# Layer 0's last results mixed into the rows beside the end of attention, seven of eight additions on POOL, and an unread Gelu behind each pair of roots

## The chip, the cores and the metric

The kernel runs on one core of a Trainium2 chip. The core has five engines, each with its own instruction queue: PE (TensorE, matrix products, with PEld for its weight loads), DVE (VectorE, elementwise and reductions), ACT (ScalarE, functions from tables and copies), POOL (GpSimd, elementwise work in SBUF and indirect DMAs), and SP (SyncE, which here only issues DMAs). An engine runs its queue in order; engines wait for each other on semaphores. The metric is the device time of one execution in microseconds (us), lower is better.

## What is computed

Two layers on 4 x 1024 rows of 256 numbers (4096 tokens), all in f32. In the reference, cut to what matters:

```
xn = layernorm(x)
s  = window attention(xn)             # 16 heads, windows of 64, relative bias, projection
g  = silu(xn + top-1 of 32 experts(xn))   # capacity 160 rows each
x  = x + s * g
xn = layernorm(x)
s  = unbind(cumsum(bind(keys, values)), query)  # unit spectra of xn Wk, xn Wv, xn Wq by FFT
g  = silu(top-2 of 8 experts(xn))     # hidden 1024, Gelu
x  = x + s * g
```

`x = x + s * g` of layer 0 and the layer norm behind it are the place of one part of the change. The other part lies where layer 1's experts (Gelu) run beside the magnitudes of the spectra (square roots).

## The kernel before

The rows lie in SBUF as 32 tiles of 128 tokens x 256, and the work between the layers goes by **quarters** of 4 tiles: there are `QUARTERS` = 8 of them, so a quarter is four tiles and not a fourth of the rows. `X` holds the rows, `XN` the normalized rows (its memory is lent to the experts' rows and down weights meanwhile), `S` the attention's output.

**The order.** `schedule0` writes one list, `plan0`, of named pieces for layer 0 and the passage to layer 1, and every engine's function walks the same list and issues its own share of each piece. What follows a product (`pt_out`, `even`, `odd`, `share`) is entered with a lag counted in PE columns (`later`), and `need` puts it in ahead of who reads it. The main loop runs over 64 window steps `s` (`STEPS`; 128 query rows each, all heads): scores for two steps at a time, `pturn(s)` (PE turns the probabilities), `pv(t)` for two steps, `proj(t)`. `side` deals the pieces of the 32 experts in between: rows turned, `gu` (gate and up products), `down`, and a `tail` for the last 32 rows of each of four experts. Their pace is set by `FIRST_EXPERT_STEP` = 9 and `LAST_EXPERT_STEP` = 62. Softmax of one step is shared out: DVE adds the bias and takes the maximum (L1509, L1513), POOL subtracts it (L2336), ACT takes Exp (L2152), DVE sums (L1523), POOL divides (L2343).

**The passage.** Each expert's result is scattered by POOL to `mixed_dram` (L2354). When all 40 scatters have landed, SP loads the mixed rows back by quarters (`mix_load`, L2531), ACT takes Silu in place (`mix_silu`, L2205), DVE multiplies by S (`mix_mul`, L1585) and adds to X (`mix_sum`, L1590). `stats` (L1349, L1351, L1354 on DVE, then a root on ACT, L2070) and `norm` (L1359, L1361, and one tile in four L1365 on DVE, three on ACT, L2215) follow. `combination` sets their order: quarter q's turn is statistics of q + 1, product and sum of q + 2, norm of q; then PE turns the quarter and starts layer 1's spectra. All of it stands behind the end of attention. Behind the last quarter comes the routing of layer 1, a chain of small operations, most of them on DVE, each waiting for the one before.

**Layer 1.** `schedule1` writes `plan1`: 39 slots of expert work (`w1`, L1308, with Gelu by chunk on ACT, L2284; `w2`, L1318), one or two tiles of 128 rows each; the slots of one tile stand among the first. Beside them go the 16 chunks of the spectra: `magnitudes` takes the root of two chunks at a time (L2258), `squares` squares the next chunk (L2251). Roots and Gelus are in different function tables, and the build puts an ACT_TABLE_LOAD ahead of the first operation that needs another table. Three PSUM banks take W1's chunks: the product of chunk c + 3 waits for the Gelu of chunk c. `gelu_table` is an unread Gelu of one column, already used once, ahead of the first slot.

Of the kernel before, what the change touches and what calls it, by code (L numbers as in the profile page):

```python
# [6 lines left out]
ALU = mybir.AluOpType  # L7
# [6 lines left out]
NT = T // P  # L14
# [116 lines left out]
UNITS, UW, UT, SR, PR0, STEPS = NT // 2, 4, 2 * P, 2, 4, 2 * NT  # L131
QUADS, RR = PAIRS // 2, 4
QUARTERS = NT // 4
EARLY_STEPS, FIRST_EXPERT_STEP, LAST_EXPERT_STEP = 8, 9, 62
NB, ROW, TOKEN, GATE = D + 1, D + 2, D, D + 1
TAIL, TAILS_AT, DOWNS, YS = CAP - P, GROUP, 6, 4
EXPERT_PIECES = GT + 2 * E0
# [71 lines left out]
def schedule0(banks):  # L209

    order = Order(banks)
# [173 lines left out]
    def spectrum(ch, n, lag):  # L385
        order.product("spectrum", ch, n, bank=spectrum_bank(ch, n), columns=0, then=[("spectrum_out", lag)])

    def combination():
        add("load_wf")
        for q in range(QUARTERS):  # L390
            add("mix_load", q)
            add("mix_silu", q)
        for q in range(2):
            add("mix_mul", q)
            add("mix_sum", q)
            if q == 0:
                add("stats", 1, 0)
        for q in range(QUARTERS):
            g = 4 * q
            if q and q % 2 == 0:  # L400
                need(("route1_turn_out", g - 8))
            if q + 1 < QUARTERS:
                add("stats", 1, g + 4)
            if q + 2 < QUARTERS:
                add("mix_mul", q + 2)
                add("mix_sum", q + 2)
            add("norm", 1, g)
            if q:
                need(("spectrum_out", *SPECTRA_AHEAD[q - 1]))
            turn(1, g, 4)  # L410
            if q % 2 == 0 and q:
                route1_turn(g - 8)
            spectrum(*SPECTRA_AHEAD[q], LATER)
            if q % 2:
                route1(g - 4)
        need(("spectrum_out", *SPECTRA_AHEAD[QUARTERS - 1]))
        route1_turn(4 * QUARTERS - 8)
        need(("route1_turn_out", 4 * QUARTERS - 8))
# [11 lines left out]
                pieces[0] += 1  # L430

    start()
    for s in range(STEPS + 4):
        u, g = divmod(s, UW)
        if s + 2 < STEPS:
            if s % 2 == 0:
                scores(s // 2 + 1)
            scored(s + 2)
        if u + 1 < UNITS and g < 3:
            (q, k, v)[g](u + 1)  # L440
        side(2 * s)
        if s % 2 == 0 and 0 <= s - 2 < STEPS:
            pv((s - 2) // 2)
        if s % 2 and 0 <= s - 3 < STEPS:
            proj((s - 3) // 2)
        side(2 * s + 1)
        if s < STEPS:
            pturn(s)
    assert next(ffn, None) is None and next(route, None) is None
    order.settle(order.clock + STEPS * UT)  # L450
    combination()
    order.settle(order.clock + STEPS * UT)
    return order.plan
# [21 lines left out]
def schedule1(banks):  # L475
# [77 lines left out]
    for n in range(NSLOT):  # L553
# [10 lines left out]
                    add("magnitudes", later)  # L564
        if ch + 2 < CHUNKS:
            spectra(ch + 2)
        for due in weights_due:
            add("load_weights", due)
        weights_due = []
# [60 lines left out]
def build(nc, a, out):  # L630
# [701 lines left out]
    def vector(e):  # L1332
        w = Waits(e)
# [68 lines left out]
        for what, *at in plan0:  # L1402
# [163 lines left out]
            elif what == "row_tokens":  # L1566
                grp, = at
                wait_rows0(w, grp)
                e.tensor_copy(row_token0[:, grp, :], rows0[:, row_slot(grp, 0):row_slot(grp, 0) + GT, TOKEN]).then_inc(
                    row_tokens_ready, 1)  # L1570
            elif what in ("y_out", "tail_out"):
                n, = at
                grp, t = divmod(n, GROUP) if what == "y_out" else (n, TAILS_AT)
                u = use["down", n] if what == "y_out" else use["tail", n]
                i = y_turn(grp, t) % YS
                rows = rows0[:, row_slot(grp, t), :]
                filled_by(u)
                w.wait_ge(y_out[i], 16 * (y_turn(grp, t) // YS))
                e.scalar_tensor_tensor(out=y0[:, i, :], in0=PS[:, u.bank, 0:D], scalar=rows[:, GATE:GATE + 1],  # L1579
                                       in1=rows[:, 0:D], op0=ALU.mult, op1=ALU.add).then_inc(free[u.bank], 1)  # L1580
            elif what == "mix_mul":
                q, = at
                four = slice(4 * q, 4 * q + 4)
                w.wait_ge(gated0, q + 1)
                e.tensor_tensor(S[:, four, :], XN[:, four, 0:D], S[:, four, :], ALU.mult).then_inc(scaled0, 1)  # L1585
            elif what == "mix_sum":
                q, = at
                four = slice(4 * q, 4 * q + 4)
                w.wait_ge(scaled0, q + 1)
                e.tensor_tensor(X[:, four, :], X[:, four, :], S[:, four, :], ALU.add).then_inc(x1_ready, 1)  # L1590
# [715 lines left out]
    def gpsimd(e):  # L2306
# [11 lines left out]
        for what, *at in plan0:  # L2318
# [27 lines left out]
            elif what in ("y_out", "tail_out"):  # L2346
# [8 lines left out]
                    out=mixed_dram, out_offset=bass.IndirectOffsetOnAxis(ap=row_token0[:, grp, t:t + 1], axis=0),  # L2355
                    in_=y0[:, i, :], in_offset=None, bounds_check=T - 1, oob_is_err=False).then_inc(y_out[i], 16)

        def late_put(n, j):
            tile = 2 * (n - EARLY) + j
            w.wait_ge(late_ready, tile + 1 if n == LAST else tile - j + 2)  # L2360
            wait_stored(w, QUARTERS)
            w.wait_ge(selected, 2)
            e.indirect_dma_start(
                out=out, out_offset=bass.IndirectOffsetOnAxis(ap=put_of[:, tile:tile + 1], axis=0), in_=fin[:, tile, 0:D],
                in_offset=None, bounds_check=T - 1, oob_is_err=False).then_inc(late_stored, 16)
# [294 lines left out]
```

## Time and profile before

| | us |
|---|---|
| median of 3 timed runs | 1129.23 (1128.43 to 1129.9) |
| the profiled execution, its own time | 1124.32 |
| its span in the trace | 1122.5 |

| engine | busy us | share of the span |
|---|---|---|
| PE | 1027.6 | 92% |
| PEld | 883.9 | 79% |
| DVE | 692.4 | 62% |
| ACT | 531.8 | 47% |
| POOL | 404.1 | 36% |

The mean granted clock of PE is 0.968 of full speed. Times within the trace count from the span's start. Attention of layer 0 with its experts ends at about 418 us, the passage to layer 1 at about 475, routing at about 545; the rest is layer 1's experts and spectra. A row of a timeline gives start, duration, engine, line, operation, what it writes and reads, how many instructions were merged, and in brackets the idle time before it with what ended it. Durations overlap a little, since an engine takes up an instruction before the one ahead has quite ended.

### The profile page before, as it was taken

The numbers are of one execution on the slowest core, as the hardware profiler recorded it, in microseconds if no ns is written. First come the engines' busy times: TensorE is split into PE (matmuls) and PEld (weight loads), VectorE is DVE, ScalarE is ACT, GpSimd is POOL, SyncE is SP. The second block draws the span as 40 slices with busy tenths as digits, with TensorE's granted clock in tenths as the row PEclk, the third lists the DMA queues.
The fourth block names the chain that finished last, engine by engine and source line by source line (L and its number), as shares of the span: only waits on it lengthen the run. The fifth ranks groups of instructions, "written<-read, shape, count | busy, mean of one in ns | idle before, by whom it ended". The sixth has DMA issues, their size and how long they took to land.

```text
span 1122.5 us, 16791 instructions
## 1 busy us (share of the span) xinstructions
PE 1027.6 (92%) x6152; PEld 883.9 (79%) x6152; DVE 692.4 (62%) x1488; ACT 531.8 (47%) x1101; POOL 404.1 (36%) x385
## 2 busy tenths in 40 slices
PE   3876999999999984789999999999999999999995
PEld 2665788888888863578888898988888888888884
DVE  7777876777777759588845644474765200058853
ACT  4624655555555536743444545455453223356531
POOL 1056545454555440000243322332231245522364
PEclk9969999999999996987999999999999999999998
DMA  9932345546565338426496855544234579989971
GB/s 307 287 136 81 94 134 164 171 133 190 179 210 174 103 109 264 157 93 254 98 350 241 290 188 187 185 171 188 108 130 191 213 269 340 338 294 389 390 285 63
DMA packets 120401, 228.65 MB, mean 204 GB/s; under 512 B 14938, under 2 KB 103914, under 8 KB 115328
## 3 DMA queue, kind: packets, MB, share of 16 engines
q1 hardware_dynamic: 106448, 189.31, 48.7%
q0 software_dynamic: 13872, 38.27, 10.3%
q8 instruction: 49, 0.80, 0.3%
q14 instruction: 32, 0.26, 0.1%
HBM read 166.98 MB, written 62.79 MB: 205 GB/s over the span
## 4 chain that ended last, share of the span: by engine, by line
PE 72%; DVE 14%; ACT 5%; issue 3%; POOL 2%; DMA 2%; SPq 0%; POOLq 0%; DVEq 0%; ACTq 0%
PE PS L1318 20%; PE PS L1308 20%; PE PS L1207 6%; PE PS L1092 4%; PE PS L1042 4%; PE PS L1146 3%; PE PS L1217 2%; PE PS L1173 2%; PE PS L1101 2%; PE PS L1159 2%; PE PS L1184 2%; POOL table L2327 2%; DVE stats L1349 2%; PE PS L1294 1%; DVE hot_tile L1831 1%
## 5 line engine op out<-in xcount | busy, mean ns | idle before, releaser
L1308 PE MATMUL PS<-xgT,WE 128*128 128x256 f32 (+1 forms) x1248 | 254.7, 361 | 5.0 <-ACT hT L2284 4.3
L2284 ACT ACTIVATE hT<-PS,WE 128x256 f32<-128x256 f32 (+1 forms) x312 | 140.2, 455 | 227.0 <-PE PS L1308 224.1
L1308 PEld LDWEIGHTS PS<-xgT,WE 128*128 128x128 f32 x1248 | 219.3, 190 | 33.3 <-ACT hT L2284 6.6
L1318 PE MATMUL PS<-WE,hT 128*128 128x256 f32 x1104 | 244.6, 379 | 0.0
L1318 PEld LDWEIGHTS PS<-WE,hT 128*128 128x128 f32 x1104 | 207.4, 190 | 27.0
L1943 DVE TENSOR_TENSOR y<-PS,WE 128x512 f32<-128x512 f32 (+1 forms) x38 | 24.3, 640 | 211.1 <-PE PS L1318 211.1
L2384 POOL DMA_INDIRECT xg<-xn_dram,token_of x71 | 74.2, 1045 | 136.9 <-DVE result_of L1859 115.1
L2396 POOL DMA_INDIRECT result<-y,result_of x53 | 53.7, 1013 | 175.7 <-DVE y L1943 168.5
L1042 PE MATMUL PS<-XT,Wf 128*128 128x256 f32 x384 | 91.6, 393 | 3.3 <-ACT Z L2061 3.3
L1042 PEld LDWEIGHTS PS<-XT,Wf 128*128 128x128 f32 x384 | 73.7, 197 | 14.6 <-ACT Z L2061 4.9
L2343 POOL TENSOR_TENSOR prob<-prob,row_sum 128x512 f32<-128x512 f32 x56 | 58.6, 1046 | 59.5 <-DVE row_sum L1525 59.2
L1207 PE MATMUL PS<-rowsT,wgu 128*128 128x160 f32 x512 | 75.6, 301 | 0.0
L2336 POOL TENSOR_TENSOR sc<-sc,sc_max 128x512 f32<-128x512 f32 x56 | 58.5, 1046 | 42.5 <-DVE sc_max L1513 42.1
L1207 PEld LDWEIGHTS PS<-rowsT,wgu 128*128 128x128 f32 x512 | 71.9, 190 | 2.3 <-issue 1.4
L1092 PE MATMUL PS<-XT,qkv_w 128*128 128x256 f32 x256 | 65.6, 402 | 0.0
L1031 PE MATMUL PS<-const,XN 128*128 128x128 f32 x128 | 27.0, 347 | 40.2 <-DVE XN L1365 38.1
L2372 POOL TENSOR_TENSOR MAG<-SQ 128x768 f32<-128x768 f32 x13 | 25.3, 1945 | 99.0 <-ACT SQ L2251 99.0
L1523 DVE TENSOR_REDUCE row_sum<-prob 128x8 f32<-128x512 f32 x64 | 43.5, 680 | 28.0 <-ACT prob L2152 27.3
L1031 PEld LDWEIGHTS PS<-const,XN 128*128 128x128 f32 x128 | 18.0, 171 | 50.1 <-issue 21.7
L2354 POOL DMA_INDIRECT mixed_dram<-y,row_token x40 | 39.7, 993 | 47.4 <-DVE y L1579 42.9
L1092 PEld LDWEIGHTS PS<-XT,qkv_w 128*128 128x128 f32 x256 | 48.6, 200 | 8.1 <-issue 0.6
L2162 ACT ACTIVATE PT<-PS 128x512 f32<-128x512 f32 x64 | 38.4, 600 | 32.2 <-PE PS L1159 31.1
(280 smaller groups left out, 1714.4 us busy)
## 6 DMA issues: line engine op xcount, KB each, us to landing
WE<-in_experts SPq DMA_DIRECT2D x39, 2180.0 KB, 9.7
wgu<-in_w_gate SPq DMA_DIRECT2D x32, 256.0 KB, 2.9
wgu<-in_w_up SPq DMA_DIRECT2D x32, 256.0 KB, 3.2
wdn<-in_w_down SPq DMA_DIRECT2D x32, 256.0 KB, 3.9
result<-zeros SPq DMA_DIRECT2D x16, 512.0 KB, 5.0
xs<-late_dram SPq DMA_DIRECT2D x16, 512.0 KB, 13.5
both<-result SPq DMA_DIRECT2D x16, 512.0 KB, 8.3
table<-zeros POOLq DMA_DIRECT2D x1, 5160.0 KB, 31.1
```

The costliest lines, as they stand in the source:

```text
L1031: m = e.transpose(out_v[:, k, j * P:(j + 1) * P], XN[:, 2 * pair + j, k * P:(k + 1) * P], ident)
L1042: m = e.matmul(PS[:, u.bank, part * CH:(part + 1) * CH], Wf[:, n, k, part * P:(part + 1) * P], XT1[:, ch, k, :], start=k == 0, stop=k == K ...
L1092: m = e.matmul(PS[:, u.bank, c * UT:(c + 1) * UT], qkv_w[:, k, col:col + P], XT0[:, unit, k, :], start=k == 0, stop=k == KD - 1)
L1207: m = e.matmul(PS[:, u.bank + f, n * CAP:(n + 1) * CAP], wgu0[:, ex % 2, n, k, f * P:(f + 1) * P], rowsT[:, grp % 2, k, j * CAP:(j + 1) * ...
L1308: m = e.matmul(PS[:, FIRST_H_BANK + nth % HR, 0:rows], W1[n % WR][:, k, c * P:(c + 1) * P], xgT[:, n % 2, k, 0:rows], start=k == 0, stop=k ...
L1318: m = e.matmul(PS[:, u.bank, j * D:(j + 1) * D], hT[:, n % 2, c, j * P:(j + 1) * P], W2[n % WR][:, c, :], start=c == 0, stop=c == KF - 1)
L1523: e.tensor_reduce(row_sum[:, s % RR, :], prob[:, s % PR0, :, :], AX.X, ALU.add).then_inc(row_sum_done, 1)
L2284: e.activation(hT[:, n % 2, c, 0:rows], PS[:, FIRST_H_BANK + (KF * n + c) % HR, 0:rows], ACT.Gelu_apprx_tanh, bias=b1[n % WR][:, c:c + 1], ...
L2336: e.tensor_tensor(by_head, by_head, sc_max[:, s % SR, :].unsqueeze(2).to_broadcast([P, PAIRS, WIN]), ALU.subtract).then_inc(sc_sub_done, 1)
L2343: e.tensor_tensor(prob[:, s % PR0, :, :], prob[:, s % PR0, :, :], row_sum[:, s % RR, :].unsqueeze(2).to_broadcast([P, PAIRS, WIN]), ALU.mu ...
L2384: e.indirect_dma_start(out=xg[:, n % XR, j, :], out_offset=None, in_=xn_dram, in_offset=bass.IndirectOffsetOnAxis(ap=token_of[:, tile:tile ...
L2396: e.indirect_dma_start(out=result1, out_offset=bass.IndirectOffsetOnAxis(ap=result_of[:, tile:tile + 1], axis=0), in_=y1[:, n % YR, j, :], ...
```

## The change

The pace of the experts ends at step 60 in place of 62. The loads of the mixed rows, their Silus, the first quarter's product, sum and statistics, and the second quarter's product move into a new function, `attention_end`, which lies around the last `proj`, `pv` and `proj`. DVE adds quarter 0 alone; POOL adds quarters 1 to 7, behind its last work of layer 0. `gelu_table` is put behind the squares of each odd `ch` from 3 to 15, seven times.

```
-EARLY_STEPS, FIRST_EXPERT_STEP, LAST_EXPERT_STEP = 8, 9, 62
+EARLY_STEPS, FIRST_EXPERT_STEP, LAST_EXPERT_STEP = 8, 9, 60
...
-    def combination():
+    def attention_end():
         add("load_wf")
         for q in range(QUARTERS):
             add("mix_load", q)
+        proj(NT - 2)
+        need(("pt_out", STEPS - 1))
+        add("mix_silu", 0)
+        pv(NT - 1)
+        need(("even", NT - 1))
+        for q in range(1, QUARTERS):
             add("mix_silu", q)
-        for q in range(2):
-            add("mix_mul", q)
-            add("mix_sum", q)
-            if q == 0:
-                add("stats", 1, 0)
+        need(("odd", NT - 1))
+        add("mix_mul", 0)
+        add("mix_sum", 0)
+        add("stats", 1, 0)
+        proj(NT - 1)
+        need(("s_out", NT - 1))
+        add("mix_mul", 1)
+        add("mix_sum", 1)
+
+    def combination():
...
+        if ch % 2 and 1 < ch < CHUNKS:
+            add("gelu_table")
...
             elif what == "mix_sum":
                 q, = at
+                if q:
+                    continue
...
+        for q in range(1, QUARTERS):
+            four = slice(4 * q, 4 * q + 4)
+            w.wait_ge(scaled0, q + 1)
+            w.wait_ge(x1_ready, q)
+            e.tensor_tensor(X[:, four, :], X[:, four, :], S[:, four, :], ALU.add).then_inc(x1_ready, 1)
```

The main loop now ends at step 63 and not four steps later, and nothing is settled between it and `attention_end`. Line numbers of the changed kernel are 12 to 20 higher than before in the engines' functions.

**PE at the end of attention.** 1217 or 1229 is the down product, 1227 or 1239 the tail, 1159 or 1171 a `pturn`, 1173 or 1185 a `pv`, 1184 or 1196 a `proj`. Before, from the last `pturn` ahead of the tail on:

```order
L1159 MATMUL PS<-const,prob 128x128 x4
L1173 MATMUL PS<-PT,VB 64x2x64 x8
L1217 MATMUL PS<-wdn_111,hT_109 128x256 x2
L1227 MATMUL PS<-wdn_111,hT_109 32x256 x8
L1159 MATMUL PS<-const,prob 128x128 x4
L1184 MATMUL PS<-proj_w,OT 128x256 x2
L1159 MATMUL PS<-const,prob 128x128 x4
L1173 MATMUL PS<-PT,VB 64x2x64 x8
L1184 MATMUL PS<-proj_w,OT 128x256 x2
```

And now:

```order
L1229 MATMUL PS<-wdn_111,hT_109 128x256 x2
L1239 MATMUL PS<-wdn_111,hT_109 32x256 x8
L1171 MATMUL PS<-const,prob 128x128 x4
L1196 MATMUL PS<-proj_w,OT 128x256 x2
L1171 MATMUL PS<-const,prob 128x128 x4
L1185 MATMUL PS<-PT,VB 64x2x64 x8
L1171 MATMUL PS<-const,prob 128x128 x8
L1196 MATMUL PS<-proj_w,OT 128x256 x2
L1185 MATMUL PS<-PT,VB 64x2x64 x8
L1196 MATMUL PS<-proj_w,OT 128x256 x2
```

Two `pturn`s, a `proj` and a `pv` that stood ahead of the last down product now stand behind the tail.

**POOL at the same place.** Before, its last work of layer 0 was:

```order
L2354 DMA mixed_dram<-y_102,row_token_52 4096x256
L2336 TENSOR_TENSOR sc<-sc,sc_max 128x512
L2343 TENSOR_TENSOR prob<-prob,row_sum 128x512 x2
L2354 DMA mixed_dram<-y_102,row_token_52 4096x256 x3
L2384 DMA xg<-xn_dram,token_of 128x256 x7
```

And now:

```order
L2350 TENSOR_TENSOR sc<-sc,sc_max 128x512
L2368 DMA mixed_dram<-y_102,row_token_52 4096x256 x2
L2350 TENSOR_TENSOR sc<-sc,sc_max 128x512
L2357 TENSOR_TENSOR prob<-prob,row_sum 128x512 x2
L2376 TENSOR_TENSOR X<-X,S 128x1024 x7
L2404 DMA xg<-xn_dram,token_of 128x256 x7
```

The last two scatters stand ahead of the last subtraction and the last two divisions, and the seven sums follow these.

**DVE in one turn of the loop over quarters** (the product of one quarter up to the statistics of the same). Before:

```order
L1585 TENSOR_TENSOR S<-XN,S 128x1024
L1590 TENSOR_TENSOR X<-X,S 128x1024
L1359 RECIPROCAL rstd<-rstd 128x4
L1361 SCALAR_TENSOR_TENSOR shift<-mean_var,rstd 128x4
L1365 TENSOR_SCALAR XN<-X,mean_var,rstd 128x256
L1349 BN_STATS stats<-X 128x6
```

And now:

```order
L1597 TENSOR_TENSOR S<-XN,S 128x1024
L1371 RECIPROCAL rstd<-rstd 128x4
L1373 SCALAR_TENSOR_TENSOR shift<-mean_var,rstd 128x4
L1377 TENSOR_SCALAR XN<-X,mean_var,rstd 128x256
L1361 BN_STATS stats<-X 128x6
```

The sum is gone from DVE, and the statistics behind the norm now read what POOL has added.

## Rows read from the trace of the kernel before

**Rows 1.** Stages: from:to, length, busy us of each engine (instructions), granted clock, DMA share, GB/s
```profile
445.00:455.00 10.00, 7.99 (x50) 5.26 (x50) 9.56 (x27) 6.53 (x16) 0.00 (x0) 1.00 0.62 211
...
570.00:850.00 280.00, 273.31 (x1430) 242.09 (x1429) 157.98 (x295) 134.03 (x273) 88.11 (x76) 1.00 0.55 201
```

**Rows 2.** Timeline of PE, end of attention: start, duration, line, operation, count, idle time before
```profile
409.02 1.10 PE L1173 MATMUL PS<-PT,VB 128*64 128x128 f32 x16 [0.69 <-ACT PT L2162]
...
412.11 0.66 PE L1159 MATMUL PS<-const,prob 128*128 128x128 f32 x4
412.60 1.03 PE L1184 MATMUL PS<-proj_w,OT 128*128 128x256 f32 x4
413.47 0.60 PE L1159 MATMUL PS<-const,prob 128*128 128x128 f32 x4
```

**Rows 3.** Timeline of POOL: the last steps' softmax, and the last scatter
```profile
405.72 1.05 POOL L2336 TENSOR_TENSOR sc<-sc,sc_max 128x512 f32<-128x512 f32 x1
...
408.93 1.04 POOL L2343 TENSOR_TENSOR prob<-prob,row_sum 128x512 f32<-128x512 f32 x1 [1.16 <-DVE row_sum L1525]
...
413.74 0.97 POOL L2354 DMA_INDIRECT mixed_dram<-y,row_token  x1 [0.30 <-issue]
```

**Rows 4.** Timeline of ACT: end of attention, first Silu, root of the last quarter
```profile
412.80 0.60 ACT L2162 ACTIVATE PT<-PS 128x512 f32<-128x512 f32 x1 [2.16 <-PE PS L1159]
...
415.90 0.48 ACT L2172 ACTIVATE OT<-PS,const 128x256 f32<-128x256 f32 x1 [1.19 <-PE PS L1173]
416.39 1.28 ACT L2205 ACT_TABLE_LOAD   x1
420.48 1.06 ACT L2205 ACTIVATE XN<-XN 128x1024 f32<-128x1024 f32 x1 [2.80 <-DMA XN<-mixed_dram]
...
465.99 0.20 ACT L2070 ACTIVATE rstd<-rstd 128x4 f32<-128x4 f32 x1
```

**Rows 5.** Timeline of DVE, the loop over quarters: quarters 0, 1 and 7
```profile
421.56 1.22 DVE L1585 TENSOR_TENSOR S<-XN,S 128x1024 f32<-128x1024 f32 x1 [3.03 <-ACT XN L2205]
...
424.08 0.43 DVE L1349 BATCH_NORM_STATS2 stats<-X 128x6 f32<-128x256 f32 x1
...
426.42 1.22 DVE L1585 TENSOR_TENSOR S<-XN,S 128x1024 f32<-128x1024 f32 x1
...
457.93 1.22 DVE L1585 TENSOR_TENSOR S<-XN,S 128x1024 f32<-128x1024 f32 x1
...
460.32 0.17 DVE L1359 RECIPROCAL rstd<-rstd 128x4 f32<-128x4 f32 x1
```

**Rows 6.** Two-input operations on POOL: the page's costliest groups, then line 2372 (min/median/max)
```profile
L2336 POOL TENSOR_TENSOR sc<-sc,sc_max 128x512 f32<-128x512 f32 x56 | 58.5, 1046 | 42.5 <-DVE sc_max L1513 42.1
...
L2372 POOL TENSOR_TENSOR MAG<-SQ x13: 1793/1803/2340, 551.9 to 830.7; 128x768 f32<-128x768 f32 x13
```

**Rows 7.** Timeline of PE, W1 of two one-tile slots: with a table load, without one
```profile
590.34 1.50 PE L1308 MATMUL PS<-xgT,WE 128*128 128x128 f32 x12
592.77 2.50 PE L1308 MATMUL PS<-xgT,WE 128*128 128x128 f32 x20 [0.92 <-ACT hT L2284]
...
613.92 3.74 PE L1308 MATMUL PS<-xgT,WE 128*128 128x128 f32 x32
```

**Rows 8.** Timeline of PE, W1 of two two-tile slots: with a table load, without one
```profile
751.36 2.76 PE L1308 MATMUL PS<-xgT,WE 128*128 128x256 f32 x12
754.31 4.58 PE L1308 MATMUL PS<-xgT,WE 128*128 128x256 f32 x20 [0.20 <-ACT hT L2284]
...
772.15 7.07 PE L1308 MATMUL PS<-xgT,WE 128*128 128x256 f32 x32
```

**Rows 9.** Timeline of ACT around the Gelu table load of one slot
```profile
586.07 1.65 ACT L2251 ACTIVATE SQ<-Z 128x512 f32<-128x512 f32 x3
591.06 1.28 ACT L2284 ACT_TABLE_LOAD   x1 [3.34 <-PE PS L1308]
592.35 0.88 ACT L2284 ACTIVATE hT<-PS,WE 128x128 f32<-128x128 f32 x3
```

## What I expected, before the changed kernel ran

> **What bounds the kernel now.** I read the table of stages first, then each engine's timeline at the three places that the edit touches. In layer 1's part PE is busy 273.3 of 280 us, so there whatever makes PE wait counts in full [rows 1]. In the passage between the layers DVE is busy 9.56 of 10 us and PE, ACT and POOL are not: POOL does nothing at all there [rows 1]. DVE starts a quarter's product at 421.56, the next at 426.42 and the product of quarter 7 at 457.93, which is 5.25 us a quarter over the last six [rows 5]. Before the passage the path is a string of single events: the last scatter is issued at 413.74, the first quarter has landed and its Silu starts at 420.48 (6.74 later), and DVE's product starts 1.08 after that [rows 3, 4, 5]. Behind the passage comes the routing of layer 1, small operations that wait for each other, so a shift of the passage's end goes through to the end of the kernel.
>
> **The change, part 1: the start of the passage.** What PE does is the same, in another order. Behind the tail now also stand two `pturn`s, a `proj` and a `pv`: 2 x 0.49 (412.11 to 412.60), 0.87 (412.60 to 413.47), 1.10 and the 0.69 that this `pv` waits for ACT's copy, in all 3.64 us [rows 2]. A `pturn`'s successor starts at 412.11 right behind the tail, so the tail ends at about 412.1 - 3.6 = 408.5. The last scatter came 1.63 after the tail (412.11 to 413.74) [rows 2, 3] and so is now issued at about 410.1; the first quarter could be there at 410.1 + 6.74 = 416.8.
>
> It can't be used then. On POOL the last subtraction and the last two divisions are queued behind the two scatters. The scatter ends at about 411.1 (0.97). From the start of a subtraction to the end of the same step's division it is 405.72 to 409.97, 4.25 us [rows 3], so the last division ends at about 411.2 + 4.25 = 415.5. Then come `pturn` (PE to the start of ACT's copy: 412.11 to 412.80, 0.69) and the copy, 0.60, which end at 416.8 [rows 2, 4]. The first Silu is behind this copy on ACT and needs a table load of 1.28 [rows 4], so it starts at about 418.1, with the data long there. Behind it, and not ahead, stands `even` of the last tile, and the product on DVE is behind `odd`: 1.08 + 0.48 + 0.48 (`odd` taken at `even`'s length) [rows 4]. Product 0 starts at about 420.2, 1.4 earlier than before. Product 1 now also has the last `s_out` ahead of it, at most another 0.48: it starts at 426.42 - 1.4 + 0.5 = 425.5, 0.9 earlier. The two steps of head start shrink to that.
>
> **Part 2: a turn of the loop.** DVE gives up a sum. From the start of a product to the first statistics it was 2.52 for product and sum, so 1.26 each; the statistics up to the next product take 2.34 (424.08 to 426.42) [rows 5]. But the order on DVE is: product of q + 2, norm of q, statistics of q + 2. The statistics read the sum, which POOL can only begin when the product is done, and DVE has only the norm to do meanwhile. So a turn becomes 1.26 + P + 2.34 + about 0.1 for two hand-overs (my estimate, an idle time of some hundredths at each) = 3.70 + P, with P the time of one sum of 1024 numbers a partition on POOL. The trace has no such operation. The nearest rows: 512 numbers, one operand broadcast, 1.046 us, twice that is 2.09; and 768 numbers with two full operands, median 1.803, times 4/3 is 2.40 [rows 6]. I take the middle, 2.25. As the upper end, the slowest of the thirteen, 2.340 for 768, gives 3.12 [rows 6]. The turn is then 5.95 us in place of 5.25. The wait that replaces the sum costs more than the sum.
>
> What is queued behind that wait: all of DVE, and through it ACT's three tiles of each norm and PE's turns and spectra. One thing comes earlier: the norm of a quarter no longer has the sum ahead of it, so it stands at 2.39 - 1.26 = 1.13 behind the product (before: 457.93 to 460.32) [rows 5]. Product 7 starts at 425.5 + 6 x 5.95 = 461.2 and the norm behind it at 462.3, against 460.32: **+2.0 us**. In general the shift is 6P - 11.5: +1.0 at 2.09, +2.9 at 2.40, +7.2 at 3.12. From there on ACT and PE carry the chain, up to the root of the last quarter at 465.99 [rows 4]; its statistics are ready at 425.5 + 7 x (3.70 + P) = 467.2, still ahead of that root (465.99 + 2.0 = 468.0). Only from P = 3.1 on do they come last, and the shift is then 7P - 14.6.
>
> The Trainium skill, "GPSIMD Engine Reference", section "Elementwise — side-by-side cycle accounting", gives 4497 ns for an f32 add of 2048 numbers on POOL; half of it, an estimate, is 2.25, which is what the rows above bracket, and by the page the sum comes out as here.
>
> **Part 3: the unread Gelus.** In a slot that follows roots, the load of the Gelu table stands ahead of the first Gelu and behind its wait for PE: ACT has been idle for 3.34 us, then loads from 591.06 to 592.35 [rows 9]. PE's product of chunk 4 waits for that Gelu. In one-tile slots W1 takes 590.34 to 595.27, 4.93 us, against 3.74 without a load: 1.19 [rows 7]. In two-tile slots 751.36 to 758.89, 7.53, against 7.07: 0.46 [rows 8]. By the slots' order the seven places fall on three one-tile and four two-tile slots: 3 x 1.19 + 4 x 0.46 = **5.4 us**. The load moves behind the squares, which end at 587.7 here; load and unread Gelu (1.28 and about 0.2, by the root of four columns, 0.20) end by 589.3, ahead of the first chunk at 591.06 [rows 4, 9]. What hides it is PE's W2 ahead of the slot. If that cover were gone, each would cost what it costs now, so this part has no loss in it. PE waits for nothing else at these seven places.
>
> The Trainium skill, "ScalarE: Activation LUTs", section "What ACT_TABLE_LOAD costs", counts 1283 ns for the load and 1380 more for a drain. The row shows the Gelu start 1.29 us after the load began [rows 9], so the trace agrees with the first number and shows nothing of the second.
>
> **Part 4: the pace of the experts.** The pieces stand closer by 51/53 and PE does the same work at the same total. I put it at nothing, and keep 1 us on either side for where a `pturn` may meet a later softmax.
>
> **Sum.** +2.0 - 5.4 = -3.4 us, the span 1119.1 in place of 1122.5, the profiled execution 1120.9 in place of 1124.32. That execution was 4.9 us below the median of the timed runs; I take the difference off the median: 1129.23 - 3.4 = **1125.8**. A measurement of this kernel can tell about 0.2% (2.3 us) from no change.
>
> **Rivals.**
> *POOL's sum is quick enough to count as small.* At P = 2.09 the shift is +1.0 and the total -4.4: 1124.8. It is the lower side of the forecast, with 1 us of part 4 beyond it: 1123.8.
> *The gain of the Gelus is eaten.* If P lies between 2.44 and 3.18 (6P - 16.9 above -2.3, 7P - 20.0 below +2.3), or part 4 costs its 1 us at P = 2.3, the kernel is within 0.2%. For it: full operands cost 2.35 ns a number against 2.04 [rows 6]. At 3.12: +7.2 - 5.4 = +1.8, 1131.0.
> *The unread Gelus do nothing*, because PE's gain comes back as a wait on the spectra's chain on DVE. Then +2.0 stays: 1131.2, still within 0.2%. Against it: PE has no wait on DVE in these slots, and DVE is busy 158 of 280 us [rows 1].
> *Slower: POOL and DVE take turns at SBUF.* DVE's norm and ACT's normalization run beside POOL's sum, which has two operands from SBUF. If a sum takes twice the broadcast row's time per number, P = 4.18, the shift is 7 x 4.18 - 14.6 = +14.7 and the total +9.3: 1138.5. It decides from P = 3.18 on. Against it: the sums of squares run in slots where DVE works too, and half of the thirteen lie between 1.793 and 1.803 [rows 6]. The Trainium skill, "GPSIMD Engine Reference", section "Key points", says that POOL's SBUF interfaces are shared with DVE and contended when DVE reads two SBUF operands; the loop has such an operation on DVE only while POOL has no sum, so by that rule the sums would be little disturbed.
>
> **How the numbers follow.** The forecast (P up to 2.44, Gelus pay) 0.56. Within 0.2%: P up to 3.18 or part 4 against me 0.20, Gelus that do nothing 0.12. Slower 0.12. So faster 0.56, same 0.32, slower 0.12. The range goes from 1123.8 less a little, 1123.6, to the case of the idle Gelus, 1131.2; the slow case is left out, with a few hundredths below.
>
> **What would show it.** In the new profile: POOL's seven sums and their mean (2.25 by me, and which P decides); DVE's products 5.95 us apart with an idle time of 1.5 to 1.7 in each turn that ends with POOL; first product at 420.2 and not 418; the first Silu behind a table load at 416.8; the norm behind product 7 at 462.3. In layer 1 no table load at the Gelus' line, and W1 at 3.74 and 7.07 in all slots. I am wrong if the turn stays below 5.3 us, if the last divisions on POOL don't hold back the Silu, or if PE shows a new wait in the slots.

## The result, and the profile after

The changed kernel is slower: a median of 1136.82 us (7 runs, 1132.95 to 1139.95) against 1128.71 for the kernel before, taken beside it (7 runs), a ratio of 1.0076 with a 95% interval of [1.006, 1.0092]. I had forecast 1125.8 and a range of 1123.6 to 1131.2. Its profiled execution took 1135.17 us, with a span of 1133.4 in place of 1122.5, so the two traces differ by 10.9 us.

The table says where, worked out from starts and ends in the two traces. "Expert" is PE's first product of layer 0's experts (L1207, after L1219), "tail" the end of the last tail (L1227, after L1239), "product" DVE's S<-XN,S of a quarter, "routing" the first operation of layer 1's routing.

| stretch, us | before | after | difference | forecast |
|---|---|---|---|---|
| start to first expert | 134.13 | 133.97 | -0.2 | 0 |
| first expert to tail | 278.05 | 279.80 | +1.75 | -3.6 |
| tail to product 0 | 9.38 | 14.38 | +5.0 | +2.3 |
| product 0 to product 1 | 4.86 | 5.18 | +0.3 | +0.4 |
| product 1 to product 7 | 31.51 | 37.16 | +5.65 | +4.2 |
| product 7 to routing | 17.66 | 19.63 | +2.0 | -1.25 |
| routing to the end | 646.91 | 643.28 | -3.6 | -5.4 |

The table of stages, from:to, length, busy us of PE, PEld, DVE, ACT and POOL (instructions), granted clock, DMA share, GB/s, to be held against [rows 1]:

```profile
445.00:455.00 10.00, 7.71 (x43) 5.07 (x41) 9.69 (x19) 4.65 (x12) 4.26 (x2) 0.88 0.50 173
570.00:850.00 280.00, 276.32 (x1461) 246.32 (x1460) 158.25 (x299) 139.25 (x287) 89.05 (x77) 1.00 0.55 202
```

DVE gave up a sum in each turn and is as busy as before, 9.69 of 10 us; its instructions in the window fall from 27 to 19. A busy engine that issues fewer instructions spends longer in some of them. In layer 1's part PE goes from 273.31 to 276.32 busy: there the unread Gelus did what was said of them.

**The end of the attention**, first PE, then POOL, then ACT, in the changed kernel (start, duration, engine, line, operation, count, idle time before and what ended it), to be held against [rows 2 to 4]:

```profile
412.70 1.07 PE L1239 MATMUL PS<-wdn,hT 128*32 128x256 f32 x16
413.71 0.66 PE L1171 MATMUL PS<-const,prob 128*128 128x128 f32 x4
...
416.35 1.09 PE L1185 MATMUL PS<-PT,VB 128*64 128x128 f32 x16 [0.69 <-ACT PT L2176]
418.73 0.66 PE L1171 MATMUL PS<-const,prob 128*128 128x128 f32 x4 [1.28 <-POOL prob L2357]
422.67 1.11 PE L1171 MATMUL PS<-const,prob 128*128 128x128 f32 x4 [3.28 <-POOL prob L2357]
423.57 1.91 PE L1196 MATMUL PS<-proj_w,OT 128*128 128x256 f32 x4
```

```profile
415.63 0.97 POOL L2368 DMA_INDIRECT mixed_dram<-y,row_token  x1 [0.30 <-issue]
416.62 1.06 POOL L2350 TENSOR_TENSOR sc<-sc,sc_max 128x512 f32<-128x512 f32 x1
417.62 1.05 POOL L2357 TENSOR_TENSOR prob<-prob,row_sum 128x512 f32<-128x512 f32 x1
421.57 1.04 POOL L2357 TENSOR_TENSOR prob<-prob,row_sum 128x512 f32<-128x512 f32 x1 [2.90 <-DVE row_sum L1537]
```

```profile
419.42 0.60 ACT L2176 ACTIVATE PT<-PS 128x512 f32<-128x512 f32 x1 [1.46 <-PE PS L1171]
419.92 0.62 ACT L2166 ACTIVATE prob<-sc 128x512 f32<-128x512 f32 x1
423.82 0.60 ACT L2176 ACTIVATE PT<-PS 128x512 f32<-128x512 f32 x1 [3.28 <-PE PS L1171]
424.43 1.28 ACT L2219 ACT_TABLE_LOAD   x1
425.73 1.06 ACT L2219 ACTIVATE XN<-XN 128x1024 f32<-128x1024 f32 x1
```

POOL's subtraction for the last step waits behind two scatters, as I had worked out. What I had not seen is on ACT: the Exp that follows it (419.92) is ready at 417.7 and stands behind the copy of the step before (419.42), which waits for a `pturn`, which waits for the division of that step. From the start of a subtraction to the end of its step's division it took 4.25 us [rows 3] and takes 5.99 here (416.62 to 422.61). PE has nothing else left, idles for 1.28 and 3.28 us, and then works slower: a `pturn` of four goes from 0.66 to 1.11, a `proj` from 1.03 to 1.91. The granted clock was 0.70 from 418 to 423 us and 0.62 from 423 to 428, between its two levels, full speed at 2.4 GHz and half of it at 1.2.

**A turn of the loop.** DVE from one product to the next, and POOL's sum beside it, to be held against [rows 5]:

```profile
439.33 1.22 DVE L1597 TENSOR_TENSOR S<-XN,S 128x1024 f32<-128x1024 f32 x1
440.47 0.17 DVE L1371 RECIPROCAL rstd<-rstd 128x4 f32<-128x4 f32 x1
440.67 2.32 DVE L1373 SCALAR_TENSOR_TENSOR shift<-mean_var,rstd 128x4 f32<-128x4 f32 x1
442.91 0.40 DVE L1377 TENSOR_SCALAR XN<-X,mean_var,rstd 128x256 f32<-128x256 f32 x1
443.23 0.41 DVE L1361 BATCH_NORM_STATS2 stats<-X 128x6 f32<-128x256 f32 x1
...
445.55 1.22 DVE L1597 TENSOR_TENSOR S<-XN,S 128x1024 f32<-128x1024 f32 x1
```

```profile
440.63 2.34 POOL L2376 TENSOR_TENSOR X<-X,S 128x1024 f32<-128x1024 f32 x1 [3.67 <-DVE S L1597]
```

The product is followed by an operation on four numbers a partition that takes 2.32 us; the sum on POOL starts 0.04 before it and ends at 442.97, with it (442.99). The turn is 6.22 us. The seven sums take 2.337 to 2.354 us. The norm, held back with the shift, still stands ahead of the statistics when the sum has ended (442.97), so these start 0.26 us behind it, at 443.23. POOL's own line says that DVE waited for it once, for 2.5 us; in the other six turns the wait is inside the four-column operation, where a table of waits doesn't show it.

**The unread Gelus.** ACT around one of the seven in the changed kernel, and PE's W1 of the two slots behind it, to be held against [rows 7 to 9]:

```profile
602.15 1.65 ACT L2265 ACTIVATE SQ<-Z 128x512 f32<-128x512 f32 x3
603.82 1.28 ACT L2268 ACT_TABLE_LOAD   x1
605.12 0.20 ACT L2268 ACTIVATE shift<-shift 128x1 f32<-128x1 f32 x1
607.16 1.18 ACT L2298 ACTIVATE hT<-PS,WE 128x128 f32<-128x128 f32 x3 [1.84 <-PE PS L1320]
```

```profile
606.43 3.74 PE L1320 MATMUL PS<-xgT,WE 128*128 128x128 f32 x32
...
613.89 7.07 PE L1320 MATMUL PS<-xgT,WE 128*128 128x256 f32 x32
```

Load and unread Gelu are over 1.1 us before W1 begins, and W1 runs through in 3.74 and 7.07 us.

### The profile page after: what moved, and what is told of

The parts are those of the page before. It is cut to its first block, busy times and chain, and to the rows that moved or that the text cites. A ratio compares the mean times of both kernels' runs of the same rounds, so it can differ in the third digit from the quotient of the medians.

```text
span 1133.4 us, 16797 instructions
## 1 busy us (share of the span) xinstructions
PE 1030.8 (91%) x6152; PEld 886.7 (78%) x6152; DVE 697.5 (62%) x1481; ACT 534.5 (47%) x1108; POOL 419.8 (37%) x392
## 4 chain that ended last, share of the span: by engine, by line
PE 70%; DVE 15%; ACT 4%; issue 4%; POOL 4%; DMA 2%; SPq 1%; POOLq 0%; DVEq 0%; ACTq 0%
PE PS L1320 20%; PE PS L1330 20%; PE PS L1219 5%; PE PS L1054 4%; PE PS L1104 3%; PE PS L1158 2%; POOL table L2341 2%; PE PS L1113 2%; PE PS L1229 2%; PE PS L1185 2%; PE PS L1196 2%; PE PS L1171 2%; DVE stats L1361 1%; DVE shift L1373 1%; PE PS L1306 1%
## 5 line engine op out<-in xcount | busy, mean ns | idle before, releaser
L1054 PE MATMUL PS<-XT,Wf 128*128 128x256 f32 x384 | 94.5, 402 | 3.3 <-ACT Z L2075 3.3
L1219 PE MATMUL PS<-rowsT,wgu 128*128 128x160 f32 x512 | 75.6, 301 | 0.0
L1219 PEld LDWEIGHTS PS<-rowsT,wgu 128*128 128x128 f32 x512 | 72.0, 190 | 2.4 <-issue 1.4
```

What stands on the lines that cost most here:

```text
L1054: m = e.matmul(PS[:, u.bank, part * CH:(part + 1) * CH], Wf[:, n, k, part * P:(part + 1) * P], XT1[:, ch, k, :], start=k == 0, stop=k == K ...
L1219: m = e.matmul(PS[:, u.bank + f, n * CAP:(n + 1) * CAP], wgu0[:, ex % 2, n, k, f * P:(f + 1) * P], rowsT[:, grp % 2, k, j * CAP:(j + 1) * ...
```

## The experiments

Three questions: which part costs what; what holds DVE beside POOL's sums; and whether POOL's help can pay in another order. The measure in the traces is the **passage**, from the tail's end to the first routing operation: 63.41 us before, 76.35 after. It does not contain the start of the program, which varies: the first expert product stands between 134 and 144 us in the traces, so spans and times contain a difference that none of the edits made.

### The Gelus alone, the pace alone, POOL's sums alone

```
# gelu_only: the kernel before, and
+        if ch % 2 and 1 < ch < CHUNKS:
+            add("gelu_table")
# pace_only: the kernel before, and
-EARLY_STEPS, FIRST_EXPERT_STEP, LAST_EXPERT_STEP = 8, 9, 62
+EARLY_STEPS, FIRST_EXPERT_STEP, LAST_EXPERT_STEP = 8, 9, 60
# pool_only: the kernel before, "if q: continue" in DVE's mix_sum, and the loop of seven sums on POOL
```

> The kernel before with the seven unread Gelus alone. Theory: they pay in full also here, 5.4 us (3 x 1.19 + 4 x 0.46) less than before, with W1 at 3.74 us in one-tile slots and 7.07 in two-tile slots, and no table load at the Gelus' line. Rival: the gain seen behind the changed passage is owed to another state of the spectra there, and alone they give back 1 us or nothing.

> The kernel before with the experts' pace at step 60 alone; the passage stays behind all of attention. Theory: the denser pieces make PE wait in mid-attention (rows not yet landed, OT, keys), about 3 to 5 us more idle time between 95 us and the tail than before, and because attention also ends on softmax steps without experts' work to lie beside, the passage starts 3 to 6 us later. Rival: the pace costs nothing, the last scatter goes out 3 us earlier than before, and all that was lost at the end of attention comes from the new order of Silu and attention.

> The kernel before with the sums of quarters 1 to 7 on POOL alone. Theory: products of the loop stand 6.23 us apart in place of 5.25, as in the changed kernel, product 7 comes 5.9 later, and with the later norm behind it the passage ends 7 to 8 us later; the DVE operation that makes the shift takes 2.3 us in each turn, as long as the sum beside it. Rival: the loop's price hangs on the early start (DMAs of the mixed rows still landing), and here it is under 3 us.

| against 1127.83 before | median us | ratio, 95% | passage | routing to the end |
|---|---|---|---|---|
| Gelus | 1123.04 | 0.9966 [0.9952, 0.998] | 63.80 | 641.97 |
| pace | 1134.35 | 1.0058 [1.0042, 1.0075] | 69.85 | 648.62 |
| POOL's sums | 1138.85 | 1.0101 [1.0078, 1.0124] | 71.20 | 648.72 |

In microseconds, by the ratio and its interval: the Gelus give 3.8 [2.3, 5.4] (4.8 in the medians); the pace, which I had put at nothing, costs 6.5 [4.7, 8.5] by itself; POOL's sums cost 11.4 [8.8, 14] (11.0 in the medians). Of these 11.4 the passage shows 7.8 (71.20 - 63.41); the rest I can't place in one trace. With POOL's sums alone the same operation on four columns takes as long as in the changed kernel:

```profile
439.28 2.31 DVE L1361 SCALAR_TENSOR_TENSOR shift<-mean_var,rstd 128x4 f32<-128x4 f32 x1
```

For the pace, the waits of PE between 134 and 414 us (what, line, waited for; us in total, times, longest), in the kernel before and then with the pace alone:

```profile
PE PS L1173 <- ACT PT L2162: 0.7, 1, 0.7
PE PS L1184 <- DVE OT L1536: 0.2, 1, 0.2
PE PS L1146 <- DVE KB L1485: 0.2, 1, 0.2
```

```profile
PE PS L1184 <- DVE OT L1536: 2.0, 2, 1.3
PE PS L1192 <- DMA rows<-table: 1.9, 2, 1.4
PE PS L1146 <- DVE KB L1485: 0.4, 1, 0.4
PE PS L1184 <- DVE KB L1485: 0.3, 1, 0.3
PE PS L1092 <- ACT Q L2093: 0.2, 1, 0.2
```

From the first expert on they grow from 1.1 to 4.6 us (the last row of the second view lies ahead of it). Closer pieces ask for a gathered tile (rows<-table), for a `proj`'s input and for keys before these are there, at six places of the attention. The other part is at the end: with the tail two `pturn`s, a `proj` and a `pv` further ahead, tail to product is 15.81 us, where 9.38 and the 3.64 us of moved work would be 13.0. The changed kernel, with its own order at the end, waits for the same four things in the attention (2.0, 1.9, 0.4 and 0.4). The share of the gathered tiles is not in every execution: `after_dve` below has the same pace and none of it, and its way from the first expert to the tail is 277.58 us.

### The new end alone, and the changed kernel with the old pace

```
# end_only: attention_end and the loop to STEPS as in the changed kernel; no Gelus, sums on DVE, and
# pace_back: the changed kernel, and
-EARLY_STEPS, FIRST_EXPERT_STEP, LAST_EXPERT_STEP = 8, 9, 60
+EARLY_STEPS, FIRST_EXPERT_STEP, LAST_EXPERT_STEP = 8, 9, 62
```

> The kernel before with the loads, Silus and first products placed around the last steps of attention, the pace left at 62, all sums on DVE, no unread Gelus. Theory: with the old pace the last scatters are no earlier than before, so the start of the first product moves by at most 1 us either way, and the kernel is within 1.5 us of before. Rival: placing Silu ahead of the last attention output costs 3 us or more by itself, because the last head outputs wait behind it on ACT.

> The changed kernel with the pace put back to step 62, all else kept. Theory: the pace costs twice, by PE's waits between the first expert and the tail (4.7 us in place of 1.2) and by the two scatters that stand ahead of the last subtraction on POOL; put back, the first product comes 10.4 us behind the tail in place of 14.4 and the tail 1.3 earlier, so the kernel is 5 to 6 us faster than the changed one. Rival: the long way from the tail to the first product is owed to the Silu placed between attention's last steps, then it stays at 13 or more.

The new end alone: 1130.88 us, 1.0019 [1.0, 1.0039], passage 64.72. The changed kernel with the old pace: 1132.17 against 1128.31, 1.0029 [1.0009, 1.0049], passage 72.64 in place of 76.35. So the new end by itself costs 1.3 us in the trace (tail to product 0 10.36, product 0 to 1 5.18, since the second product now has the last `s_out` ahead of it), and by the ratio 2.1 [0, 4.4], where 1.5 at most was expected. Put back, the pace returns some 5.3 us, give or take 3 (1.0076 to 1.0029), of the 8.6 that the changed kernel lost: a large part of the loss was in the part that I gave two sentences. The prices of the four single edits don't add up to the whole: 6.5 + 11.4 + 2.1 - 3.8 = 16.2 us against 8.6. One overlap is seen in the traces: pace alone and end alone lengthen tail to product 0 by 6.4 and 1.0 us, and both together, in the changed kernel, by 5.0.

### What holds DVE: another shift, and a sum with one operand

`shift_apart` is the changed kernel with the four-column operation cut into four of one column, each with one tensor from SBUF and one number a partition. `pool_one` is the kernel before with, in place of the seven sums, a product of X with 1 on POOL; it leaves out the addition of S to quarters 1 to 7.

```
# shift_apart
-            e.scalar_tensor_tensor(out=shift[:, g:g + n], in0=mean_var[:, g:g + n, 0], scalar=-1.0, in1=rstd[:, g:g + n],
-                                   op0=ALU.mult, op1=ALU.mult).then_inc(ln_shift, 1)
+            for t in range(g, g + n):
+                m = e.tensor_scalar(shift[:, t:t + 1], mean_var[:, t, 0:1], rstd[:, t:t + 1], -1.0, ALU.mult, ALU.mult)
+            m.then_inc(ln_shift, 1)
# pool_one, against pool_only
-            e.tensor_tensor(X[:, four, :], X[:, four, :], S[:, four, :], ALU.add).then_inc(x1_ready, 1)
+            e.tensor_scalar(X[:, four, :], X[:, four, :], 1.0, None, ALU.mult).then_inc(x1_ready, 1)
```

> The changed kernel with the norm's shift made by four DVE operations that read one column each as a scalar (one SBUF operand) in place of one operation with two operands from SBUF. Theory: a DVE operation with two SBUF operands cannot start while POOL's two-operand sum runs; without it the norm ends 2 us earlier, products stand 6.0 us apart in place of 6.2 and the passage ends 3 us earlier. Rival: whatever DVE does first beside a POOL sum takes 2.3 us, or the operation waits for something else; then the first of the four takes 2.3 us and nothing moves.

> The kernel before, with POOL's seven sums replaced by a multiplication of X by 1 in place (one operand from SBUF, same size); the addition of S to quarters 1 to 7 is left out. My theory: DVE is held by POOL's two operands from SBUF. With one operand DVE's 4-column shift operation, which took 2.31 us beside a sum, takes 0.16 to 0.3, and the norm is not held; the loop's turn is 3.70 us plus the time of this POOL operation plus about 0.15. Rival: any POOL operation of that size holds DVE: then the shift operation again lasts until POOL's operation ends. Second rival: the shift operation waits for something else in the new order (a root, a semaphore): then it is 2 us again too, whatever POOL does.

DVE and POOL in the kernel with the shift apart (1136.38 us, 1.0066 [1.0046, 1.0086]):

```profile
447.77 0.58 DVE L1374 TENSOR_SCALAR shift<-mean_var,rstd 128x1 f32<-128x1 f32 x4
448.27 1.96 DVE L1378 TENSOR_SCALAR XN<-X,mean_var,rstd 128x256 f32<-128x256 f32 x1
```

```profile
447.73 2.34 POOL L2377 TENSOR_TENSOR X<-X,S 128x1024 f32<-128x1024 f32 x1 [3.67 <-DVE S L1598]
```

The shift is free of the sum (0.58 for four), and now the next operation is held, the one of 256 columns, 1.96 us where it takes 0.40 alone, though it reads one tensor of that width and two numbers a partition. So two tensors are not the only form that is held, which neither expectation had. The shift being ready sets ACT's three tiles free, and product 7 to routing is back at 17.68; the turn only falls to 6.03, since the statistics read the sum anyway. In the trace the passage gains 2.7 us (73.63); in time the two kernels can't be told apart.

And the one with a single operand on POOL, DVE first:

```profile
444.32 1.01 DVE L1361 SCALAR_TENSOR_TENSOR shift<-mean_var,rstd 128x4 f32<-128x4 f32 x1
445.26 0.40 DVE L1365 TENSOR_SCALAR XN<-X,mean_var,rstd 128x256 f32<-128x256 f32 x1
```

```profile
444.29 2.77 POOL L2364 TENSOR_SCALAR X<-X 128x1024 f32<-128x1024 f32 x1 [3.67 <-DVE S L1585]
```

Neither expectation holds as written. The operation is held for 0.85 us and let go 1.7 us before POOL has ended, and the norm behind it takes its usual 0.40 with POOL still at work. So the hold depends on what POOL does, and it is no semaphore and no root; but one operand on POOL also holds DVE for a while. Why just so long stays open, and so does whether the number of operands decides or the kind of operation, since the run changed both. The turn, 3.70 us plus POOL's time, comes out here: 3.70 + 2.77 = 6.47, measured 6.45 (38.67 / 6). Beside the sums it is 6.19 and not 6.04: there the held norm delays the statistics. In time this kernel is 1148.46 against 1137.14, 1.009 [1.006, 1.012]; its rows are other ones behind the passage, so only the loop is read from it.

### The changed kernel with its sums back on DVE

```
# after_dve: the changed kernel without "if q: continue" and without the seven sums on POOL
```

> The changed kernel with all sums on DVE again (pace 60, the new end of attention and the seven Gelus stay). My theory: the turn of the loop goes back from 6.19 to 5.25 us and the norm behind product 7 is not held, so 5.65 + 2.0 = 7.6 us come back: about 1129.2 against the 1136.8 of the changed kernel, within 0.2% of the kernel before; what stays is the pace and the new end (+6.5) against the Gelus (-5). Rival: the longer turn comes from the later start of the passage or from the order around it, not from POOL: then the product 0 to product 7 stretch stays at 42 us and the time above 1134.

1136.59 us against 1137.14, 0.9996 [0.9977, 1.0015] (`after_dve`, `pool_one` and `ahead_dve_gelu` ran on another chip, where the kernel before takes 1137.14 us, so only their ratios are compared). The changed kernel stands at 1.0076, so in it POOL's sums cost about 0.8%, 9 us, give or take 3. The turn is 5.25 us again and product 7 to routing 17.67, which gives back the 7.6 expected. The passage is 69.43 in place of 76.35, 6.9 us less, since tail to product 0 is 0.7 longer in this trace. What stays against the kernel before is the pace and the end, +6.0 in the passage; in time the Gelus about pay for it.

### The loop in another order, with POOL's sums and without

The turn is long because the statistics of a quarter stand right behind its sum. Here a quarter's product is issued three quarters ahead and its statistics one turn later, so that POOL adds while DVE does another quarter's statistics. Start, pace and end of attention are those of the kernel before, and the Gelus are in.

```
-        for q in range(2):
+        for q in range(3):
             add("mix_mul", q)
             add("mix_sum", q)
-            if q == 0:
-                add("stats", 1, 0)
+            if q:
+                add("stats", 1, 4 * q - 4)
...
-            if q + 1 < QUARTERS:
-                add("stats", 1, g + 4)
-            if q + 2 < QUARTERS:
-                add("mix_mul", q + 2)
-                add("mix_sum", q + 2)
             add("norm", 1, g)
+            if q + 3 < QUARTERS:
+                add("mix_mul", q + 3)
+                add("mix_sum", q + 3)
...
             spectrum(*SPECTRA_AHEAD[q], LATER)
+            if q + 2 < QUARTERS:
+                add("stats", 1, g + 8)
```

`ahead_gelu` has the sums on POOL, `ahead_gelu_shift` also the shift apart, `ahead_dve_gelu` has all sums on DVE.

> The kernel before with the unread Gelus and POOL's sums, but the loop reordered: norm of q, product of q + 3, statistics of q + 2, so that a sum lies beside statistics of another quarter. Theory: statistics have one SBUF operand and are not held by POOL's sum, and no one waits for the sum; a turn takes 1.2 + 0.6 + 2.3 = 4.1 to 4.4 us in place of 5.25, the passage ends about 5 us earlier than before, and with the Gelus the kernel is 9 to 11 us faster than before. Rival: statistics stretch beside the sum as the shift does, a turn stays above 5.2 us and only the Gelus' 5.4 us are left.

> As the reordered kernel with the unread Gelus, and the shift from four operations with one SBUF operand each. Theory: the sum ends about when the statistics do, so there is little left to free; within 1 us of the other. Rival: sums still overlap the next norm by 0.5 us or more a turn, then this one is 2 to 4 us faster.

> The reordered loop (product two quarters further ahead, statistics a quarter behind the sum) with all sums on DVE, and the seven Gelus. My theory: DVE is the bound of the loop, so without POOL's help the turn stays at about 5.25 us whatever the order, products 1 to 7 take 31.5 us and the time is that of the Gelus alone, 1122 to 1124: the gain of 4.3 us of the reordered loop with POOL's sums comes from the sums that DVE doesn't do. Rival: the order alone does it (statistics further from the norm, ACT and PE less late): then turns near 4.7 us or a time of 1119 to 1120.

| | median us | before | ratio, 95% | product 1 to 7 | passage |
|---|---|---|---|---|---|
| sums on POOL | 1118.76 | 1128.31 | 0.9923 [0.9908, 0.9938] | 26.94 | 58.97 |
| and shift apart | 1121.40 | 1128.31 | 0.9943 [0.993, 0.9957] | 29.01 | 59.67 |
| sums on DVE | 1130.77 | 1137.14 | 0.9936 [0.9912, 0.996] | 31.50 | 63.25 |

One turn of the first, DVE and POOL:

```profile
440.98 0.16 DVE L1363 SCALAR_TENSOR_TENSOR shift<-mean_var,rstd 128x4 f32<-128x4 f32 x1
441.06 0.41 DVE L1367 TENSOR_SCALAR XN<-X,mean_var,rstd 128x256 f32<-128x256 f32 x1
441.38 1.22 DVE L1587 TENSOR_TENSOR S<-XN,S 128x1024 f32<-128x1024 f32 x1
442.52 0.42 DVE L1351 BATCH_NORM_STATS2 stats<-X 128x6 f32<-128x256 f32 x1
...
445.19 0.16 DVE L1363 SCALAR_TENSOR_TENSOR shift<-mean_var,rstd 128x4 f32<-128x4 f32 x1
...
445.59 1.22 DVE L1587 TENSOR_TENSOR S<-XN,S 128x1024 f32<-128x1024 f32 x1
```

```profile
442.68 2.37 POOL L2366 TENSOR_TENSOR X<-X,S 128x1024 f32<-128x1024 f32 x1 [1.84 <-DVE S L1587]
```

This turn is 4.21 us (4.49 on average, since the second of the six is 6.57). The statistics run beside the sum at their usual 0.4 us, and the shift falls behind its end, at 0.16. There the shift apart has nothing to free and only adds: four operations take 0.58 us where one takes 0.16, the turn is 4.62, and products 1 to 7 take 2.1 us longer, where I had expected the two kernels within 1 us. With the sums on POOL and the shift whole this is the version that beats both kernels: 9.6 us below the kernel before, and by the intervals better than the Gelus alone (0.9952 to 0.998). The expected 9 to 11 us came, with 4.4 of passage. In the traces the order alone brings 0.5 us of passage (63.80 to 63.25) and POOL's sums in it another 4.3 (58.97). The times don't show that split: the intervals with and without POOL overlap, and the two ran on different chips.

## Why the prediction was wrong

**Where PE, DVE and POOL stand** (what bounds the kernel now): right. DVE bounds the passage, and its shift goes through to the end.

**Part 1, the start of the passage: wrong by 8.1 us**, from the first expert to product 0: 279.80 + 14.38 = 294.18, where I had 420.2 - 134.13 = 286.07. I named the queue on POOL rightly: last scatter 1.86 us behind the tail (1.63 said), the divisions held back, the Silu behind the last copy and a table load. Three terms were missing or too small. From the first expert the tail comes 5.4 us later than I said: 3.5 are PE's new waits, which belong to part 4, 0.9 is a `proj` that stood ahead of the first expert and now stands behind it, and 1.0 I can't place. The step of 4.25 from subtraction to division was read from a place where ACT was free; here the Exp was queued behind a copy that waited for PE: +1.75. And I priced PE's last pieces at full clock: from the end of the division to product 0 it is 5.54 us (422.61 to 428.15) in place of 4.7, because the copy starts 1.15 behind its `pturn` and not 0.69, and `even` waits 0.46 for the slower `pv`. The chain of one step must be read with what stands ahead of each of its links on its own engine.

**Part 2, the loop.** The turn, 3.70 + P with P = 2.25, came out as 6.19 with P = 2.34: nearly right in form (3.70 + 2.34 is 6.04, the held norm makes the rest), and 1.5 us too small over six turns, within the bounds I had. The term that failed is the one behind it: "the norm of a quarter no longer has the sum ahead of it, so it stands at 1.13 behind the product". It stands 3.58 behind (439.33 to 442.91), because DVE's shift is held for as long as POOL adds. That turned a gain of 1.25 us into a loss of 2.0. This was to be read before the run: in the trace of the kernel before, DVE and then POOL at two places of layer 1 where both read two tensors from SBUF:

```profile
551.83 0.42 DVE L1894 TENSOR_TENSOR PR<-Z 128x256 f32<-128x256 f32 x1
552.16 2.03 DVE L1895 TENSOR_TENSOR PR<-Z 128x256 f32<-128x256 f32 x1
...
746.22 0.68 DVE L1898 TENSOR_TENSOR Z<-Z,MAG 128x512 f32<-128x512 f32 x1
746.83 2.30 DVE L1903 TENSOR_TENSOR_SCAN RUN<-PR,RUN 128x256 f32<-128x256 f32 x1
```

```profile
551.89 2.02 POOL L2372 TENSOR_TENSOR MAG<-SQ 128x768 f32<-128x768 f32 x1 [12.58 <-ACT SQ L2251]
...
746.24 2.33 POOL L2372 TENSOR_TENSOR MAG<-SQ 128x768 f32<-128x768 f32 x1 [7.34 <-ACT SQ L2251]
```

The same form takes 0.42 and, beside POOL, 2.03 us; the scan takes 0.72 without POOL and 2.30 with it. Of the thirteen sums on this line five have a DVE instruction beside them, and in all five DVE is held past the sum's end. The sum pays too where DVE was first: 2.33 us in place of 1.80 where it starts 0.02 us behind a DVE product (746.24 against 746.22), three times. In the eight sums of 1.79 to 1.80 us DVE did nothing at all. So my argument against the slower rival, that half of the thirteen take 1.793 to 1.803 in slots where DVE works too, stood on sums with no DVE beside them, and the 2.340 that I took for the upper end of P was a sum that had to wait. In the loop POOL's sum starts 0.04 us ahead of the shift, and the shift waits.

The Trainium skill, "GPSIMD Engine Reference", section "Key points", names contention with DVE instructions in a 2-port perf mode or with two SBUF inputs. The four-column shift has two, it stands right in the sum's time, and the runs bear the rule out for it; I had quoted this half and then wrongly said that the loop has no such instruction beside a sum. Whether the TENSOR_SCALAR of 256 columns that is held in `shift_apart` is a case of the other half, no run here shows.

**Part 3, the unread Gelus: right.** 5.4 us said; 3.74 and 7.07 in the seven slots as said, no table load at the Gelus' line. Alone they give 4.8 us in the medians, 3.8 [2.3, 5.4] by the ratio. Routing to the end is 641.97 us with the Gelus alone and 643.28 in the changed kernel, against 646.91 to 648.72 in four kernels without them; that the changed kernel shows -3.6 and not -5.4 lies in this spread. On the slower chip it is 646.15 and 646.46 in two kernels with them.

**Part 4, the pace: wrong, "nothing, with 1 us on either side".** It costs 5.3 us in the changed kernel and 6.5 alone, an error as large as that of the sums, which cost 9.0 and 11.4 in time where my loop and norm came to 3.0 (4.2 - 1.25). The work on PE was the same, but what feeds it was not ahead by more than the two steps taken away: +3.5 us of waits in the attention and about 3 at its end.

**Sum and rivals.** Said -3.4, traces +10.9: part 1 +8.1, loop +1.5, product 7 to routing +3.2, routing to the end +1.8 make 14.6 us; less 0.3 for the start and product 1 that is the 14.3 between the two. The slower rival was the right place with the wrong victim: I let POOL's sum grow to 4.18 us, and it stayed at 2.34. No rival had a pace that costs more than 1 us. With the four parts priced by the single edits a loss would have been the likeliest.

## What to carry over

Before work goes to POOL, look in the trace for the longest instance of each of DVE's operations, not its mean, and at what POOL did in that time, and for POOL's operations the other way round; then place the moved work beside operations that aren't held, as the statistics here. Work that is moved ahead of another step must be followed through every engine's queue, link by link, since one copy that waits holds back the Exp behind it. A table of pace is an edit like any other: it costs what the engine's suppliers are late by, and where PE is at 99% no supplier has been shown to be early.

## What the runs showed of the hardware

- DVE's four-column operation with two SBUF tensors takes 0.16 us alone, 2.32 beside a POOL sum with two, and 1.01 beside a POOL product with one. A 256-column TENSOR_SCALAR goes from 0.40 to 1.96 beside such a sum and stays at 0.40 beside the product. Statistics (0.4 us) and TENSOR_SCALARs of one or four columns (0.58 for four, and 0.3) are not held to the sum's end.
- In these traces the one that starts second waits: POOL's sum of 768 takes 2.33 us in place of 1.80 where a DVE product with two SBUF tensors started 0.02 us ahead of it, and DVE's shift takes 2.32 in place of 0.16 where POOL's sum started 0.04 us ahead.
- A POOL operation on 1024 numbers with one operand took 2.77 us, longer than the sum of two at 2.34.
- At the end of attention in the changed kernel, where PE was without work for 1.28 and 3.28 us, its granted clock was 0.70 (418 to 423 us) and 0.62 (423 to 428). Later in the loop, with PE waiting more in each turn, it was 0.98, 0.85 and 0.83 in the three stretches of 10 us from 448 on, against 1.00 before (442 to 472).
